# A two-layer sequence model on one core: block turns moved in front of the sums' emptying, value spreads in one pass of 128 rows, and a longer TensorE loop

## The chip, the cores and the metric

The kernel runs on one core of a Trainium2 chip. The metric is the device time of one execution in microseconds (us). The engines are TensorE (PE; its weight loads are PEld), VectorE (DVE), ScalarE (ACT), GpSimd (POOL) and SyncE (SP), which here only issues DMAs. Differences of less than 0.2% can't be told from no change.

## The reference, cut to what matters

`x` is 8 batches of 512 tokens of 128 numbers. Layer 0 adds a pairwise attention of 16 channels and a routed expert block to `x`; layer 1 adds a linear attention with a hierarchical state and a gated feed-forward block:

```
xn = layernorm(x)
# layer 0, for each of 16 channels c of 64 numbers:
u, v = xn @ U.T * s, xn @ V.T * s
q    = sigmoid(u_c @ v_c.T)                 # 512 x 512 scores
G    = concat(q @ v_c) @ U + concat(q.T @ u_c) @ V, times s
F    = for 8 experts: the 64 tokens with the best router logit,
       attention among them, added back at their places
x    = x + G + F
xn = layernorm(x)
# layer 1
k, q = elu(xn Wk)+1, elu(xn Wq)+1 ;  v = xn Wv
y    = sum over 7 groups of features f: D_f(q) * cumsum_t( A_f(k) * B_f(v) )
x    = x + (y / denominator) @ Wo
       + (silu(xn Wg) * (xn Wu)) @ Wd
```

A, B, C and D are multiplications by fixed 64 x 128 matrices ("spreads"): B spreads the values v. Products that must be exact are made from a high and a low part (`fp32r`): high x high, high x low, low x high.

## The kernel before, in words

A prologue loads and normalises all batches, computes the router logits and picks the tokens (0 to 88 us), then runs the experts (88 to 158 us). The first pair of channels of batch 0 is computed by itself in that time ("early").

The main part walks over batches. A batch is 8 pairs of channels (`j`), a pair is two halves (`o` = 0 and 1), so 16 halves, h = 0 to 15; even halves have `o` = 0. In each half TensorE does, in this order:

1. `scores`: four units, each 6 passes on 64 rows (u times v, 24 matmuls, two at a time on the two halves of the array), into eight PSUM banks. ACT turns each unit into `tanh` (L1172). Before the fourth unit TensorE waits (`s_oe`) until DVE has emptied the other sum's bank: in an odd half that is the sum of the even half just before.
2. the middle work, by a table: in even halves the next pair's u and v (`pu`, `pv`, 3 passes each) and the output projection of the last pair (`pj`, 6 passes); and steps of layer 1 of the batch before: the spreads (`ROWS`) and single steps (`FULL_STEPS`, both in the table at L69 to L75). A spread B stands alone in halves 4, 5 and 6 (`B0`, `B1`, `B2`), and beside a D later.
3. `weighted`: four units of `tok` times `tanh`, 16 fp32 matmuls, into the sum's bank (`o_bank`), which DVE then empties as high and low part (`evac_o`, L866 and L868).

`tok` is u and v of the pair with tokens on the partitions. It is made from `raw` (u and v, copied by ACT, L1121) by a DVE transposition of 32 x 32 blocks (`turn`, L789) into the single buffer `blocks`, and by 16 DMAs from SP that put the blocks in their places (`move_tokens`, L533). `turn` waits until the DMAs of the turn before have landed (`s_moved`), and the first `weighted` of the next pair waits for its own. In an even half the turn stands in DVE's order behind the emptying of that half's sum, which needs the last `weighted` of the half.

Batch 0 runs without layer 1 (halves 2 to 15) as straight code, batches 1 to 7 in a loop of one batch a pass (`pe.Fori(1, B)`), and then comes the tail: layer 1 of the last batch. The first pair that the main part needs (`turn(0, 0)`) goes the same way through a buffer of its own, `first_blocks`, at 155 us.

A second buffer name to know: layer 1's gate uses `tg`, which shares its place with `kexp` (the exponential of the step `kq`).

Of the kernel before, what the change touches and what calls it, by code (L numbers as in the profile page):

```python
# [35 lines left out]
ALU = mybir.AluOpType  # L36
# [3 lines left out]
P = 128  # L40
B, T, D = 8, 512, 128
TB = T // P
# [31 lines left out]
FULL_STEPS = {1: [("back", 0)], 2: [("norm", 0)], 3: [("kq", 0), ("v", 0)], 12: [("down", 0)], 15: [("yo", 0), ("yo", 1)]}  # L74
FULL_STEPS |= {h: [("gate", f), ("up", f)] for h, f in ((5, 0), (6, 1), (9, 2))}  # L75

# [124 lines left out]
def prep_index(g, k):  # L201


    return g * 2 + 3 + k
# [6 lines left out]
def build(nc, io):  # L211
    ctx = ExitStack()
    with ctx:
# [17 lines left out]
        def scatter_bank(i):  # L231
            return x_bank(("sc", 0), not isinstance(i, int))
# [18 lines left out]

        mv1, ve1, rstd1 = sb("mv1", [P, B, TB, 2]), sb("ve1", [P, B, TB]), sb("rstd1", [P, B, TB])
# [70 lines left out]
        wr_b = take_upper(B * (E * B + 1))  # L323
# [34 lines left out]
        first_blocks = view(arena[:, at[0] - 6 * T:at[0] - 4 * T], (2, T))  # L358
# [18 lines left out]
        later_blocks = sb("blocks", [P, 2, T])  # L377
# [17 lines left out]
        s_stats, s_rstd = sem("stats_ready"), sem("rstd_ready")  # L395
        s_xn, s_xT, s_xnT = sem("xn_ready"), sem("xn_transposed"), sem("xn1T_ready")
# [88 lines left out]
        def _(sp):  # L485
# [42 lines left out]
            def move_tokens(i, j, blocks):  # L528

                sp.wait_ge(s_turned, i * PAIRS + j + 1)  # L530
                for r in range(QUARTERS):
                    for a in range(QUARTERS):
                        sp.dma_start(tok[32 * r:32 * r + 32, (j + 1) % 2, :, :, 32 * a:32 * a + 32].rearrange("t w k c -> t (w k) c"),  # L533
                                     blocks[32 * a:32 * a + 32].rearrange("t w (k r c) -> t (w k) r c", k=TB, r=QUARTERS)[:, :, r])\
                          .then_inc(s_moved[j], 16)

            move_rows(E - 2, E // 2 - 1, 0)
            move_tokens(0, 0, first_blocks)
            move_rows(E - 1, E // 2 - 1, 1)

# [9 lines left out]
            load_rows(0)  # L550
            for j in range(1, PAIRS):
                move_tokens(0, j, later_blocks)
                if j == 2:
                    sp.wait_ge(s_yp, 1)
                    load_rows(1)

            def batch(n, more):
                for j in range(PAIRS):
                    move_tokens(n, j, later_blocks)
# [67 lines left out]
        def _(dve):  # L627
# [52 lines left out]
            def part_rows(h):  # L680
                dve.wait_ge(s_rstd, h + 1)
                for n in range(h * X_PART, (h + 1) * X_PART):
                    if n >= 2:
# [1077 lines left out]
```

## Time and profile before

| | us |
|---|---|
| median of 3 runs | 1463.75 (1462.65 to 1465.48) |
| the profiled execution | 1468.4 |
| its span (first to last instruction) | 1466.6 |
| batch 0, from the first score of half 2 | 157.93 to 294.93 |
| seven passes of the loop | 294.93 to 1413.70, 158.7 to 161.9 each |
| tail | 1413.70 to 1466.6 |

TensorE is busy in 95% of the span, DVE in 62%, ACT in 47%. Times in the rows are from the span's start. An idle time in brackets stands in front of the group it belongs to, and behind the arrow is what ended it; "issue" means that no other engine was waited for. Matmul ends are modelled, so the distance from start to start tells what a pass costs.

### The profile page before, as it was taken

The page shows a single profiled execution, that of the slowest core. Times are in us where ns is not written, and L with a number is a line of the kernel's source. Part 1 is how long each engine was busy: PE and PEld are TensorE (multiplying, and loading weights), DVE is VectorE, ACT ScalarE, POOL GpSimd, SP SyncE. Part 2 cuts the span into 40 slices and gives each one's busy share as a digit, 9 for nine tenths or more (in the row PEclk, how much of TensorE's full clock was granted, in tenths as well). Part 3 has the DMA queues.
Part 4 walks back from the last instruction along what each step waited for, and adds up shares of the span by engine and source line. Part 5 has one row for each costly group of instructions (what it writes and reads, how often), then busy time and mean ns, then how long its engine had stood idle before and what let it go on. Part 6 is the DMA issues. An engine that isn't in the chain of part 4 may idle for free.

```text
span 1466.6 us, 24503 instructions
## 1 busy us (share of the span) xinstructions
PE 1389.9 (95%) x7806; PEld 793.9 (54%) x7806; DVE 903.6 (62%) x1559; ACT 688.9 (47%) x1058; POOL 44.1 (3%) x41
## 2 busy tenths in 40 slices
PE   6999798899998999999999999999999999999968
PEld 3566444455564555555565555555655555555534
DVE  8868443366655665656655656556555666566657
ACT  3556344444443544454444543454544454454421
POOL 4000400000000000000000000000000000000000
PEclk9999899999999999999999999999999999999988
DMA  6012222112221212221112211221212111221110
GB/s 207 1 31 66 43 35 31 26 29 35 30 30 31 33 27 30 36 32 31 26 26 39 36 29 24 36 34 28 30 29 36 32 26 27 38 30 27 25 30 8
DMA packets 302620, 51.37 MB, mean 35 GB/s; under 512 B 280545, under 2 KB 300769, under 8 KB 302465
## 3 DMA queue, kind: packets, MB, share of 16 engines
q1 hardware_dynamic: 302128, 47.82, 19.4%
q8 instruction: 78, 1.28, 0.4%
q0 software_dynamic: 336, 1.64, 0.3%
q14 instruction: 78, 0.63, 0.2%
HBM read 11.64 MB, written 4.19 MB: 11 GB/s over the span
## 4 chain that ended last, share of the span: by engine, by line
issue 85%; DVE 1%; PE 1%; POOL 1%; ACT 0%; POOLq 0%; DVEq 0%
PE psum L1231 1%; DVE arena L917 0%; DVE arena L923 0%; DVE arena L915 0%; POOL u_w_hl L608 0%; POOL v_w_hl L608 0%; POOL rstd_s L623 0%; POOL up_hl L608 0%; DVE arena L939 0%; PE psum L1575 0%; DVE xn_s L663 0%; POOL u_w_hl L605 0%; POOL v_w_hl L605 0%; DVE x_all L932 0%; POOL up_hl L605 0%
## 5 line engine op out<-in xcount | busy, mean ns | idle before, releaser
L1172 ACT ACTIVATE arena<-psum 128x1024 f32<-128x1024 f32 x504 | 476.0, 1030 | 636.5 <-PE psum L1231 636.3
L1231 PE MATMUL psum<-arena 128*64 128x512 f32 x2016 | 466.0, 605 | 26.0 <-DMA arena<-blocks 14.6
L1231 PEld LDWEIGHTS psum<-arena 128*64 128x64 f32 x2016 | 135.0, 138 | 290.0 <-issue 244.7
L1231 PE MATMUL psum<-u_parts,v_parts 64*128 64x512 f32 x1536 | 199.5, 404 | 11.9 <-issue 11.2
L1231 PE MATMUL psum<-v_parts,u_parts 64*128 64x512 f32 (+1 forms) x1568 | 201.9, 397 | 0.0
L866 DVE TENSOR_SCALAR o_hl<-psum,sums 128x512 fp32r<-128x512 f32 x126 | 94.4, 749 | 162.1 <-PE psum L1231 162.1
L1231 PEld LDWEIGHTS psum<-u_parts,v_parts 64*128 64x128 f32 x1536 | 141.7, 187 | 93.1 <-issue 45.3
L1231 PEld LDWEIGHTS psum<-v_parts,u_parts 64*128 64x128 f32 (+1 forms) x1568 | 145.3, 184 | 81.5 <-issue 51.1
L868 DVE SCALAR_TENSOR_TENSOR o_hl<-psum,sums,o_hl 128x512 fp32r<-128x512 f32 x126 | 94.6, 751 | 4.5
L1121 ACT ACTIVATE arena<-psum 128x512 f32<-128x512 f32 x128 | 77.1, 625 | 18.5 <-PE psum L1231 18.5
L923 DVE TENSOR_TENSOR arena<-psum,arena 128x512 f32<-128x512 f32 x96 | 64.6, 689 | 33.7 <-PE psum L1231 31.7
L772 DVE CAST u_parts<-arena 128x512 fp32r<-128x512 f32 x64 | 28.7, 448 | 88.0 <-ACT arena L1121 88.0
L789 DVE STREAM_TRANSPOSE blocks<-arena 128x1024 f32<-128x1024 f32 x63 | 77.8, 1234 | 0.0
L917 DVE TENSOR_TENSOR_SCAN arena<-ones,arena 128x512 f32<-128x512 f32 x56 | 68.6, 1224 | 1.9
L915 DVE TENSOR_TENSOR arena<-psum,arena 128x512 f32<-128x512 f32 x32 | 22.1, 691 | 63.0 <-PE psum L1231 36.4
L1231 PE MATMUL psum<-sel_r,uT_hl 128*128 128x512 f32 x189 | 60.5, 428 | 0.0
L1231 PE MATMUL psum<-o_hl,u_w_hl 128*128 128x512 f32 x189 | 54.0, 394 | 1.7 <-DVE o_hl L868 1.7
L1231 PE MATMUL psum<-sel_r,vT_hl 128*128 128x512 f32 x189 | 54.5, 396 | 0.0
L1231 PE MATMUL psum<-o_hl,v_w_hl 128*128 128x512 f32 x189 | 53.2, 389 | 0.0
L1231 PE MATMUL psum<-arena,top_w 128*64 128x512 f32 x96 | 49.3, 595 | 1.5 <-DVE arena L923 1.5
L1231 PE MATMUL psum<-arena,bot_w 128*64 128x512 f32 x96 | 49.3, 595 | 0.0
L773 DVE TENSOR_TENSOR u_parts<-arena,u_parts 128x512 fp32r<-128x512 f32 x64 | 46.5, 727 | 2.2
(211 smaller groups left out, 1517.0 us busy)
## 6 DMA issues: line engine op xcount, KB each, us to landing
arena<-blocks SPq DMA_DIRECT2D x1008, 32.0 KB, 2.0
x_all<-in_x SPq DMA_DIRECT2D x4, 512.0 KB, 5.4
upper<-in_we SPq DMA_DIRECT2D x8, 256.0 KB, 2.7
expert_rows<-upper SPq DMA_DIRECT2D x16, 128.0 KB, 2.5
xn_s<-expert_rows SPq DMA_DIRECT2D x8, 256.0 KB, 2.9
out<-x_all SPq DMA_DIRECT2D x8, 256.0 KB, 2.5
arena<-in_e POOLq DMA_DIRECT2D x1, 896.0 KB, 5.7
arena<-in_wi POOLq DMA_DIRECT2D x1, 576.0 KB, 5.7
```

Of the source, the lines that this page charges most:

```text
L772: link(nc.vector.tensor_copy(hl[:, par, 0], raw[:]))
L773: return nc.vector.tensor_tensor(hl[:, par, 1], raw[:], hl[:, par, 0], ALU.subtract)
L789: nc.vector.transpose(blocks.rearrange("p w t -> p (w t)"), raw.rearrange("p w t -> p (w t)")).then_inc(s_turned, 1)
L866: nc.vector.tensor_scalar(o_hl[:, o, 0], o_bank[o][:], total, None, ALU.add).then_inc(s_oh, 1)
L868: nc.vector.scalar_tensor_tensor(o_hl[:, o, 1], o_bank[o][:], total, o_hl[:, o, 0], ALU.add, ALU.subtract)\
L915: nc.vector.tensor_tensor(ab[:], bk[:], bs_of(f)[:], ALU.mult).then_inc(s_ld, 1)
L917: link(nc.vector.tensor_tensor_scan(pre[:], ones[:], ab[:], 0.0, ALU.mult, ALU.add))
L923: nc.vector.tensor_tensor(pc[half][:, r % 2], bk[:], pre[:], ALU.mult).then_inc(s_ld, 1)
L1121: nc.scalar.activation(raw[:], bk[:], ACT.Copy, accum_out=total[:, par:par + 1]).then_inc(s_prep_free, 1)
L1172: nc.scalar.activation(th_of(un), psum[:, at:at + 2], ACT.Tanh, scale=0.5 * FACTOR_SCALE ** 2).then_inc(s_th, 2)
L1231: return nc.tensor.matmul(out, lhsT, rhs, start=start, stop=stop)
```

## The change

Seven edits go together.

1. In an even half `turn` now stands in front of `evac_o`.
2. The two tiles of the first pair of the main part are made by eight TensorE transpositions (`prep` with k = 3 and 4) and two ACT copies (`prep_tok`) instead of `turn(0, 0)` and 16 DMAs; `first_blocks` goes.
3. A lone B spread is one pass over 128 rows: the low part of v is written to rows 64 to 127 of `val_high`, whose weights are the same as those of rows 0 to 63. B2 keeps a second pass for the low part of the weights. The subtraction that makes the low part becomes two of 64 rows.
4. The first gate and up step move from half 5 to half 3, behind `kq` and `v`.
5. TensorE's loop has two batches in its body and runs three times; batch 1 is straight code in front of it. The other engines' loops stay.
6. In the prologue ACT normalises the odd batches (`odd_rows`), DVE the even ones.
7. The router logits of two batches go into column groups 0 to 31 and 64 to 95 with 32 output rows each, instead of 64 rows for one batch.

```diff
-FULL_STEPS = {1: [("back", 0)], 2: [("norm", 0)], 3: [("kq", 0), ("v", 0)], 12: ...
-FULL_STEPS |= {h: [("gate", f), ("up", f)] for h, f in ((5, 0), (6, 1), (9, 2))}
+FULL_STEPS = {1: [("back", 0)], 2: [("norm", 0)], 3: [("kq", 0), ("v", 0), ("gate", 0), ("up", 0)], 12: ...
+FULL_STEPS |= {h: [("gate", f), ("up", f)] for h, f in ((6, 1), (9, 2))}
...
             def part_rows(h):
                 dve.wait_ge(s_rstd, h + 1)
-                for n in range(h * X_PART, (h + 1) * X_PART):
-                    ...
-                    normalised(xn_g[:, n % 2], n, ...).then_inc(s_xn, 1)
+                odd, even = h * X_PART + 1, h * X_PART
+                nc.vector.scalar_tensor_tensor(shift1[:, odd], mv1[:, odd, :, 0], -1.0, rstd1[:, odd], ALU.mult, ALU.mult)\
+                  .then_inc(s_shift, 1)
+                if h:
+                    dve.wait_ge(s_xT, even - 1)
+                normalised(xn_g[:, 0], even, ...).then_inc(s_xn, 1)
...
-            def turn(i, j, blocks):
-                if not (isinstance(i, int) and i == j == 0):
-                    dve.wait_ge(s_moved[(j - 1) % PAIRS], (i + (j > 0)) * MOVED)
+            def turn(i, j):
+                if not (isinstance(i, int) and i == 0 and j == 1):
+                    dve.wait_ge(s_moved[(j - 1) % PAIRS], moved_count(i if j else i - 1, (j - 1) % PAIRS))
...
-            dve.wait_ge(s_prep_w, 1)
-            turn(0, 0, first_blocks)
             expert_rows(E - 1, 1, E // 2 - 1)
...
                 elif kind == "v":
                     dve.wait_ge(s_vh, L + 1)
-                    nc.vector.tensor_tensor(val_parts[1][:], bk[:], val_parts[0][:], ALU.subtract).then_inc(s_ld, 1)
+                    nc.vector.tensor_tensor(val_parts[0][64:128], bk[64:128], val_parts[0][64:128], ALU.subtract)
+                    nc.vector.tensor_tensor(val_parts[1][0:64], bk[0:64], val_parts[0][0:64], ALU.subtract).then_inc(s_ld, 1)
...
+                    if o == 0:
+                        if not some_before:
+                            for n in range(2):
+                                dve.wait_ge(s_ymv[n], 16 * E)
+                        turn(i, j)
                     evac_o(g, j, o, some_before)
                     for r in range(ROUNDS):
                         ...
-                    if o == 0:
-                        ...
-                        turn(i, j, later_blocks)
...
+            def odd_rows(n):
+                act.wait_ge(s_shift, n // 2 + 1)
+                if n >= 2:
+                    act.wait_ge(s_xT, n - 1)
+                for k in range(TB):
+                    ins = nc.scalar.activation(xn_g[:, 1, k], x_all[:, n, k], ACT.Identity, bias=shift1[:, n, k:k + 1],
+                                               scale=rstd1[:, n, k:k + 1])
+                ins.then_inc(s_xna, 1)
...
+            def prep_tok(k, w, bk):
+                act.wait_ge(s_prep_full, prep_index(0, k) + 1)
+                copy(tok[:, 1, w].rearrange("p k c -> p (k c)"), bk[:]).then_inc(s_prep_free, 1)
...
-                return mm(bank[2][0:E * B], wr_b[:, n * E * B:(n + 1) * E * B], xn1T[:, n], n == 0, n == B - 1)
+                for g in range(2):
+                    ins = mm(bank[2][g * 64:g * 64 + 32], wr_b[:, pair * 32:pair * 32 + 32], xn1T[:, 2 * pair + g],
+                             pair == 0, pair == B // 2 - 1)
...
+                if len(group) == 1 and group[0][0] == "B":
+                    f, bk = group[0][1], banks[0]
+                    ins = mm(bk[:], e_high[:, (NF + f) * P:(NF + f + 1) * P], val_parts[0][:], True, f < 2)
+                    if f >= 2:
+                        ins = mm(bk[:], e_low[0:64, ...], val_parts[0][0:64], False, True)
+                    ins.then_inc(s_lf, 1)
+                    return
...
             probabilities_back(*last)
+            prep(0, 3, 1, 0, bank[2])
             attend(*last)
+            prep(0, 4, 1, 0, bank[3])
             expert_out(*last)
...
-            with pe.Fori(1, B) as i:
-                iteration(i, True, True)
+            iteration(1, True, True)
+            with pe.Fori(1, B // 2) as m:
+                for n in range(2):
+                    iteration(m * 2 + n, True, True)
```

DVE's order at the end of half 4 of a batch in the loop, before (u and v parts of the next pair, the projection's sum, the emptying of the sum in two instructions, the turn):

```order
L773 TENSOR_TENSOR v_parts<-arena,v_parts 128x512
L858 SCALAR_TENSOR_TENSOR arena<-psum,arena 128x512
L863 ISA
L866 TENSOR_SCALAR o_hl<-psum,sums 128x512
L867 REGISTER_ALU
L868 SCALAR_TENSOR_TENSOR o_hl<-psum,sums,o_hl 128x512
L789 STREAM_TRANSPOSE blocks<-arena 128x1024
```

The same place with the change:

```order
L783 TENSOR_TENSOR v_parts<-arena,v_parts 128x512
L866 SCALAR_TENSOR_TENSOR arena<-psum,arena 128x512
L798 REGISTER_ALU
L799 STREAM_TRANSPOSE blocks<-arena 128x1024
L871 ISA
L874 TENSOR_SCALAR o_hl<-psum,sums 128x512
L875 REGISTER_ALU
L876 SCALAR_TENSOR_TENSOR o_hl<-psum,sums,o_hl 128x512
```

The turn is now the instruction in front of the two that empty the sum.

TensorE's order in the middle of half 5, before (from the scores' last unit to the first `weighted`):

```order
L1231 MATMUL psum<-v_parts,u_parts 128x512 x6
L1465 REGISTER_ALU
L1231 MATMUL psum<-val_high,e_high 128x512
L1231 MATMUL psum<-val_low,e_high 128x512
L1465 REGISTER_ALU
L1231 MATMUL psum<-kq_high,e_high 128x512 x2
L1231 MATMUL psum<-kq_low,e_high 128x512 x2
L1231 MATMUL psum<-sel_r,gate_hl 128x512 x3
L1465 REGISTER_ALU
L1231 MATMUL psum<-sel_r,up_hl 128x512 x3
L1231 MATMUL psum<-arena 64x512 x6
```

and with the change:

```order
L1265 MATMUL psum<-v_parts,u_parts 128x512 x6
L1509 REGISTER_ALU
L1265 MATMUL psum<-val_high,e_high 128x512
L1509 REGISTER_ALU
L1265 MATMUL psum<-kq_high,e_high 128x512 x2
L1265 MATMUL psum<-kq_low,e_high 128x512 x2
L1583 REGISTER_ALU
L1265 MATMUL psum<-arena 64x512 x6
```

The pass of `val_low` has gone, and the six passes of gate and up stand in half 3 behind those of `kq` and `v`.

## Rows read from the trace of the kernel before

**Rows 1.** The page's first part: busy us, share of the span, instructions.
```profile
PE 1389.9 (95%) x7806; PEld 793.9 (54%) x7806; DVE 903.6 (62%) x1559; ACT 688.9 (47%) x1058; POOL 44.1 (3%) x41
```

**Rows 2.** Waits of TensorE: who waited for what, us in total, times, longest.
```profile
PE psum L1231 <- DMA arena<-blocks: 14.6, 16, 2.3
...
PE psum L1231 <- issue: 11.2, 7, 2.2
...
PE psum L1231 <- DMA arena<-arena: 5.5, 1, 5.5
...
PE psum L1231 <- DVE val_low L911: 2.7, 1, 2.7
```

**Rows 3.** Timeline, half 0 of batch 4: start, us, engine, line, operation.
```profile
784.59 0.68 DVE L858 SCALAR_TENSOR_TENSOR arena<-psum,arena 128x512 f32<-128x512 f32 x1
...
787.15 0.75 DVE L866 TENSOR_SCALAR o_hl<-psum,sums 128x512 fp32r<-128x512 f32 x1 [1.87 <-PE psum L1231]
...
788.60 1.23 DVE L789 STREAM_TRANSPOSE blocks<-arena 128x1024 f32<-128x1024 f32 x1
```

**Rows 4.** Timeline of batch 3: a train of block DMAs on SP's queue.
```profile
708.10 10.86 SPq L533 DMA_DIRECT2D arena<-blocks  x16
```

**Rows 5.** Timeline of batches 0 and 2: `weighted` behind a short and two long waits.
```profile
262.83 3.65 PE L1231 MATMUL psum<-arena 128*64 128x512 f32 x16 [0.98 <-DMA arena<-blocks]
...
282.08 5.35 PE L1231 MATMUL psum<-arena 128*64 128x512 f32 x16 [2.06 <-DMA arena<-blocks]
...
462.84 4.49 PE L1231 MATMUL psum<-arena 128*64 128x512 f32 x12 [2.28 <-DMA arena<-blocks]
```

**Rows 6.** Timeline: the first scores of batches 2 and 4.
```profile
454.56 3.02 PE L1231 MATMUL psum<-u_parts,v_parts 64*128 64x512 f32 x24 [1.56 <-issue]
...
775.99 4.22 PE L1231 MATMUL psum<-u_parts,v_parts 64*128 64x512 f32 x24 [2.17 <-issue]
```

**Rows 7.** Timeline, end of half 4 of batch 4.
```profile
819.85 0.69 DVE L915 TENSOR_TENSOR arena<-psum,arena 128x512 f32<-128x512 f32 x1 [3.80 <-ACT arena L1027]
...
824.56 0.68 DVE L858 SCALAR_TENSOR_TENSOR arena<-psum,arena 128x512 f32<-128x512 f32 x1
824.83 3.03 PE L1231 MATMUL psum<-v_parts,u_parts 64*128 64x512 f32 x24
825.16 0.74 DVE L866 TENSOR_SCALAR o_hl<-psum,sums 128x512 fp32r<-128x512 f32 x1
```

**Rows 8.** Timeline of TensorE, half 8 of batch 3: passes on 64 and on 128 rows.
```profile
696.69 0.39 PE L1231 MATMUL psum<-kq_low,e_high 64*128 64x512 f32 x2
696.91 0.39 PE L1231 MATMUL psum<-kq_high,e_low 64*128 64x512 f32 x2
697.23 0.97 PE L1231 MATMUL psum<-sel_r,uT_hl 128*128 128x512 f32 x3
```

**Rows 9.** Timeline of DVE, half 3 of batch 4.
```profile
813.52 0.68 DVE L911 TENSOR_TENSOR val_low<-psum,val_high 128x512 fp32r<-128x512 f32 x1
814.51 0.75 DVE L866 TENSOR_SCALAR o_hl<-psum,sums 128x512 fp32r<-128x512 f32 x1 [0.31 <-PE psum L1231]
```

**Rows 10.** Timeline of TensorE, an odd half of batch 0 without middle work.
```profile
252.26 3.65 PE L1231 MATMUL psum<-arena 128*64 128x512 f32 x16 [0.97 <-ACT arena L1172]
```

**Rows 11.** Timeline around half 2 of batch 0, all engines.
```profile
164.08 1.91 DVE L772 CAST u_parts<-arena 128x512 fp32r<-128x512 f32 x1 [4.71 <-ACT arena L1121]
...
167.58 1.36 DVE L773 TENSOR_TENSOR v_parts<-arena,v_parts 128x512 fp32r<-128x512 f32 x1
...
168.82 5.88 PE L1231 MATMUL psum<-arena 128*64 128x512 f32 x16 [5.45 <-DMA arena<-arena]
174.63 3.06 PE L1231 MATMUL psum<-v_parts,u_parts 64*128 64x512 f32 x24
```

**Rows 12.** Timeline of the prologue: one batch's logits, and the router's exponential.
```profile
21.80 1.07 PE L1231 MATMUL psum<-xn1T,upper 128*64 128x512 f32 x2
...
26.95 0.59 ACT L1036 ACTIVATE arena<-psum 64x512 f32<-64x512 f32 x1 [1.17 <-PE psum L1231]
```

More of the change, by code:

```diff
@@ L231, in scatter_bank @@
         def scatter_bank(i):
-            return x_bank(("sc", 0), not isinstance(i, int))
+            return x_bank(("sc", 0), not (isinstance(i, int) and i == 0))
         x_all = sb("x_all", [P, B, TB, D])
@@ L527, in _ @@
                 move_rows(E - 4 + par, E // 2 - 2, par)
[L528 to L539, printed above, removed]
+            for par in range(2):
+                move_rows(E - 2 + par, E // 2 - 1, par)
             def load_rows(n):
@@ L1008, in iteration @@
                             add_y(r, i - 1)
-                    if o == 0:
-                        if not some_before:
-                            for n in range(2):
-                                dve.wait_ge(s_ymv[n], 16 * E)
-                        turn(i, j, later_blocks)
             iteration(0, True, False)
@@ L1032, in transposed @@
                 copy(xn1T[:, n], bank[par][:]).then_inc(s_xnT, 1)
-            pairs(fori_of(act), transposed)
+            def odd_rows(n):
[6 more added lines that the diff above has]
+                ins.then_inc(s_xna, 1)
+            odd_rows(1)
+            for n in range(0, B, 2):
+                transposed(n, 0)
+                transposed(n + 1, 1)
+                if n + 3 < B:
+                    odd_rows(n + 3)
             act.wait_ge(s_lg, 1)
-            nc.scalar.activation(tk_work, bank[2][0:E * B], ACT.Exp, scale=-1.0).then_inc(s_ex, 1)
+            for g in range(2):
+                ins = nc.scalar.activation(tk_work[g * 32:g * 32 + 32], bank[2][g * 64:g * 64 + 32], ACT.Exp, scale=-1.0)
+            ins.then_inc(s_ex, 1)
             act.wait_ge(s_first, 16 * len(first_consts))
@@ L1117, in prep_raw @@
                     act.wait_ge(s_us if k == 1 else s_vs_rdy, g + 1)
-                    act.wait_ge(s_turned, g)
+                    if isinstance(g, int) and g == 1:
+                        act.wait_ge(s_prep_full, prep_index(0, 4) + 1)
+                    else:
+                        act.wait_ge(s_turned, g - 1)
                 if q is not None:
@@ L1233, in _, with transposes @@
             pe.wait_ge(s_first, 16 * len(first_consts))
-            def transposes(n, par):
-                pe.wait_ge(s_xn, n + 1)
-                if later(n):
+            def transposes(n):
+                par = n % 2
+                if par == 0:
+                    pe.wait_ge(s_xn, n // 2 + 1)
+                else:
+                    pe.wait_ge(s_xna, n // 2 + 1)
+                if n >= 2:
                     pe.wait_ge(s_xnT, n - 1)
@@ L1482, in prep @@
                     ins = product(bk, uv_hl[k - 1], pair, xn1_hl)
+                else:
+                    pe.wait_ge(s_prep_free, prep_index(g, k - 2) + 1)
+                    for t in range(TB):
+                        ins = nc.tensor.transpose(bk[:, t * P:(t + 1) * P], (u_raw if k == 3 else v_raw)[:, t * P:(t + 1) * P],
+                                                  ident[:])
                 ins.then_inc(s_prep_full, 1)
```

84 lines of the change are left out of this document (51 added, 33 removed).

## The prediction

> **What bounds the kernel now.** I read the page's first part, then TensorE's waits, then the timeline of every place that the change touches. TensorE is busy in 95% of the span [rows 1]: what the change gives or takes is what it does to TensorE's passes and pauses. In the list of its waits the reader is to see four lines [rows 2]: 14.6 us in 16 waits for block DMAs, 11.2 us in 7 waits for nothing but issue (a short one in the prologue, and six at turns of the loop, some 10.9 together), one wait of 5.5 us for the first pair's DMAs, and one of 2.7 us in the tail. A wait can cost more than itself: 16 `weighted` matmuls take 3.65 us after a wait of 0.98, but 5.35 after one of 2.06, and 12 of them take 4.49 after one of 2.28 [rows 5]; the granted clock falls, to the lower of its levels at worst. The pauses that the change aims at are some 34 us, or 2.3%. What a measurement of this kernel can tell from no change is 0.2%, 3 us.
>
> **Part 1, the turn in front.** In half 0 DVE is done at 785.2 and stands idle 1.87 us for the last `weighted`, empties the sum in two instructions, and turns at 788.60 [rows 3]. The turn needs only `raw`, which was there before. In front it runs in that pause, costs TensorE nothing, and starts 3.4 us earlier. Its train of 16 DMAs takes 10.86 us to issue [rows 4] and about 2 more to land, so it ends as much earlier. The longest wait is 2.28 us [rows 5], so all 16 should go: 14.6 us, and the slow stretches behind the waits of 2.06 and 2.28 with them, 5.35 - 3.65 = 1.7 and 4.49 - 2.65 (12 matmuls at full clock) = 1.8. Term: -18.
>
> One even half is different. In half 4 DVE waits 3.80 us for ACT's copy of B0, and from there works without a pause: `add_g` starts at 824.56, the emptying 0.60 behind it at 825.16, when the half has been over since 824.83 [rows 7]. Here the turn finds no pause; it puts the two emptying instructions off by some 1.2, to end at 827.9 instead of 826.7. Behind them TensorE waits with the fourth unit of half 5. That unit begins 18 matmuls, 9 pairs of 0.227, into the half, at 826.9. So a stall of 1.0 to 1.3, I take 1.15, once in each of seven batches: +8.0. Below it can be nothing (if DVE gets ahead), above 1.5.
>
> **Part 2, the first pair on TensorE.** The wait of 5.45 us at 168.82 goes, and the slow 5.88 becomes 3.65 [rows 11]: 7.7 in all. The eight transpositions (about 0.6 us for four) stand in two gaps of 0.7 each where TensorE waits for ACT at the last expert; they cost nothing there, at worst 1.2. But something else comes late. DVE's parts of the next pair, which wait for nobody before, take 1.91 to 1.36 us each beside POOL's work and end only at 168.94 [rows 11]; the half would now end near 167. Turn and emptying stand behind them: emptied at about 171.8, while the fourth unit of half 3 wants it at 169.1. A stall of 2.7 is given back. Term: -5, between 0 and -7.7.
>
> **Part 3, the lone B.** A pass lasts 0.22 us (696.69 to 696.91) [rows 8]. Three passes a batch less would be 0.67. But a 128-row pass now stands between 64-row passes. The row shows the price of changing from 64 to 128 rows: 0.32 instead of 0.22 from 696.91 to 697.23 [rows 8]. B0 and B1 each get one such change more, and one back, which no row shows; I take the same 0.1 for it, between 0 and 0.2. They then save 0.03 each, and B2, which stands before 128-row passes anyway, 0.22: together 0.28 a batch, 2.0 in seven. The Trainium skill, "TensorEngine Tiling (Array Packing)", Key Properties, says that changing the tiling mode drains the array; by free passes the term would be 4.7, by this rule nearer to 2, and the trace's 0.1 agrees with the rule. The second subtraction on DVE is counted next.
>
> **Part 4, gate and up in half 3.** Six passes of 0.23, 1.4 us, leave half 5 and enter half 3: no change in the sum, if both halves stay filled. Half 5 then has three short passes between scores and `weighted`, about 1.1 us with the changes; an odd half with nothing there waits 0.97 for the third tanh [rows 10], so it is just full. In half 3 DVE's chain grows by three instructions. From the subtraction at 813.52 [rows 9] I count 0.6, 0.6 and 0.7 to the next starts, so up starts near 815.4 and ends near 816.1. The emptying, which started at 814.51 as soon as the half was over [rows 9], could now start at 815.9 (1.4 later) and has to wait for up until 816.1. It ends at 817.6; the fourth unit of half 4 wants it 2.04 into the half, at 817.8. The move costs nothing, and 0.5 a batch (3.5) if my count is short. Half 5's stall from part 1 isn't hidden by this. Terms of parts 3 and 4: -2.
>
> **Part 5, the longer loop.** Six turns back cost 10.9 us of pause: 1.56 and 2.17 are two of them, and behind the second the scores take 4.22 instead of 3.02 [rows 6]. With batch 1 in front and two batches a pass there are two turns back left, four go: 4 x 1.8 = 7.3, and perhaps one slow stretch (1.3). Straight code shows no such pauses: batch 0 is straight and has none between its halves. Term: -8 (7.3 and half of that stretch), between 0 and -10. A body twice as long could make each of the two turns dearer; the Trainium skill, "Runtime: NRT & Kernel Launch", Instruction fetch mechanics, says that a taken branch outside a small window forces a fetch of its target, whatever the length of the body. By that rule the price goes with the number of turns, which is what I take from the row.
>
> **Parts 6 and 7, the prologue.** From 20 us on each batch takes 1.59 us of TensorE (the next logits start 1.59 later), 1.07 of it the logits [rows 12]. Two batches' logits side by side in two column groups would take 1.07 for both. But ACT now has the odd rows too (four activations, near 1.2) and the last statistics come at 17 us and through POOL at 18.6. I follow the chain: last even rows at 20.0, odd at 21.4, copies at 22.8, logits at 24.0, two exponentials to 25.2, where it was 27.54 (26.95 + 0.59) [rows 12]. DVE's search for the best tokens and the early pair both start from there. Term: -2.5, between 0 and -4.
>
> **The tail.** TensorE waits 2.7 us for `val_low` [rows 2]; the six passes of gate and up now fill it, and 1.3 us of DVE work leave the chain behind. Against it stands one subtraction more, 0.6. Term: -1.5, between +0.7 and -3.
>
> **The sum.** -18 + 8 - 5 - 2 - 8 - 2.5 - 1.5 = -29. The profiled execution took 1468.4 (span 1466.6) and would take 1439. The runs' median is 4.65 below that execution; from 1463.75 the sum gives 1434.75, I say 1435.
>
> **Rivals.**
> *The trains stay the limit.* If the DMAs, not the turn, decide (one buffer `blocks`, trains that follow each other), only half of the 18 comes: 1444. For it: a train with its landing is 13 us of the 17 to 22 of a pair. Against it: a pause of 4 us or more between trains. 10%.
> *The chain in halves 3 to 5 is dearer.* DVE late in half 3 too (+3.5) and stalls of 1.5 (+2.4), with no gain from the lone B (+2): 1443. For it: half 4 has no slack at all [rows 7]. 15%.
> *Better.* The stall in half 5 is absorbed, and the prologue and the first pair give their full: 1435 - 8 - 1.5 - 2.7 = 1423. Against it: the chain of rows 7 is all DVE's own work. 10%.
> *Slower.* The turn stands in front of the emptying in every even half, 63 of them. If DVE came to it less than about 0.8 us before the half's end everywhere, as in half 4, TensorE's fourth unit would stall 0.95 (1.24 of turn less 0.3 of slack) in the 56 others too: +53, less my 29: 1488. It decides from the point where DVE's last work ends later than that. In half 0 it ends 1.87 before [rows 3], and only half 4 fails: 3%.
> *The longer body doesn't help* (its two turns cost as much as six): 1443. Only the total of 10.9 speaks for a fixed price. 7%.
>
> **How the numbers follow.** My forecast has 55%, with a range of its own of 1428 to 1441. The cases at 1443 and 1444 have 32%, the better one 10%, the slower 3%. Eight in ten lie between 1423 and 1448. All but the slower case and a little unknown are faster by more than 0.2%: faster 0.94, same 0.02, slower 0.04.
>
> **What would show it.** In the profile after: waits of TensorE for blocks gone or under 2 us; two waits called issue near 2 us in the loop, not six; turns that end before the emptying starts; in half 5 a gap in the scores before the fourth unit, near 1.1 us, in each batch; no wait at half 2 of batch 0, but one in half 3; the first exponential near 24; batches of about 158. I am wrong if block waits remain, if the scores of odd halves other than 5 are stretched, or if the pauses at the loop's two turns grow past 4.

## The result, and the profile after

| | before | after |
|---|---|---|
| median of 5 runs each | 1464.23 us (1462.65 to 1468.57) | 1454.76 us (1454.3 to 1455.87) |
| ratio, 95% interval | | 0.9931 (0.9917 to 0.9946) |
| span of the profiled execution | 1466.6 | 1453.3 |
| start of half 2 of batch 0 | 157.93 | 155.64 |
| batch 0 | 137.00 | 124.67 |
| from there to the last half of batch 7 | 1109.40 | 1113.09 |
| what follows | 62.27 | 59.90 |

The change gains 9.5 us, not the 29 forecast; 1454.76 lies above the forecast's own range of 1428 to 1441. The start, batch 0 and the end gain 17.0 us of the span. The loop, where seven eighths of the work are, loses 3.7. Places within the execution are read from one profiled execution of each kernel.

First the parts of the page and the list of TensorE's waits after (us in total, times, longest), which answer to [rows 1, 2]:

```profile
PE 1387.6 (95%) x7790; PEld 785.1 (54%) x7790; DVE 903.1 (62%) x1554; ACT 698.2 (48%) x1077; POOL 44.7 (3%) x41
```

```profile
PE psum L1265 <- DVE o_hl L876: 12.9, 13, 3.5
PE psum L1265 <- issue: 8.1, 5, 2.3
...
PE psum L1265 <- DVE val_low L920: 1.4, 1, 1.4
```

No wait for block DMAs is left: 14.6 and 5.5 us are gone. New is the first line, 13 waits for the sum's emptying. "issue" fell only from 11.2 to 8.1, though four of six turns of the loop went.

Half by half (start of the first score to start of the next half's), summed over batches 1 to 7 (half 15: 1 to 6), after minus before. A half 15 so ends with the pause of the turn behind it, if there is one; the six passes of gate and up that moved make nearly all of half 3's +9.54.

```
half 0: -0.92   half 1: +6.37   half 3: +9.54   half 4: +1.55   half 5: -4.16
half 6: +1.32   half 8: -3.37   half 15: -7.79
```

Four things are new in them. First, TensorE's turn of the loop in the changed kernel (timeline of TensorE at the first scores of batches 4 and 6; the idle time in front of a group stands in brackets):

```profile
758.12 0.49 PE L1265 MATMUL psum<-u_parts,v_parts 64*128 64x512 f32 x1 [2.03 <-issue]
760.86 5.22 PE L1265 MATMUL psum<-u_parts,v_parts 64*128 64x512 f32 x23 [2.24 <-issue]
...
1080.58 0.49 PE L1265 MATMUL psum<-u_parts,v_parts 64*128 64x512 f32 x1 [1.26 <-issue]
1083.34 4.46 PE L1265 MATMUL psum<-u_parts,v_parts 64*128 64x512 f32 x23 [2.27 <-issue]
```

Each turn pauses twice, with one score between, and the 23 scores behind take 5.22 and 4.46 us where 24 took 3.02 [rows 6]. The granted clock was 0.50 from 758.8 to 765.6 and from 1083.3 to 1086.4, its lower level. Half 0 of those two batches takes 14.45 and 13.71 us, of the others 9.50.

Second, half 1 of the batches in which TensorE does not turn (timeline of batch 2, DVE and then TensorE):

```profile
442.47 0.69 DVE L961 TENSOR_TENSOR arena<-xn_s,arena 128x512 f32<-128x512 f32 x1 [3.03 <-issue]
...
448.70 1.23 DVE L799 STREAM_TRANSPOSE blocks<-arena 128x1024 f32<-128x1024 f32 x1
449.86 0.71 DVE L874 TENSOR_SCALAR o_hl<-psum,sums 128x512 fp32r<-128x512 f32 x1
450.60 0.75 DVE L876 SCALAR_TENSOR_TENSOR o_hl<-psum,sums,o_hl 128x512 fp32r<-128x512 f32 x1
```

```profile
448.84 1.67 PE L1265 MATMUL psum<-v_parts,u_parts 64*128 64x512 f32 x12 [0.59 <-DVE arena L866]
451.41 0.96 PE L1265 MATMUL psum<-v_parts,u_parts 64*128 64x512 f32 x6 [0.90 <-DVE o_hl L876]
```

DVE's own loop still turns once a batch, with an idle time of 3.03 us for "issue". From there it works without a pause to the emptying of half 0's sum, and TensorE waits for it. Before, DVE had the same pause (14.8 us in six), but TensorE paused in the same place in each batch, and half 1 took 8.97 everywhere. Now it takes 11.05, 10.38, 10.36 and 10.42 in batches 2, 3, 5 and 7.

Third, the lone B. Timeline of TensorE in half 4 of batch 4, before and after, from the pass of `val_high` to the first pass on 128 rows:

```profile
817.26 0.39 PE L1231 MATMUL psum<-val_high,e_high 64*128 64x512 f32 x1
817.49 0.39 PE L1231 MATMUL psum<-val_low,e_high 64*128 64x512 f32 x1
817.55 0.56 PE L1231 MATMUL psum<-kq_high,e_high 64*128 64x512 f32 x2
817.88 0.46 PE L1231 MATMUL psum<-kq_low,e_high 64*128 64x512 f32 x2
```

```profile
804.32 0.50 PE L1265 MATMUL psum<-val_high,e_high 128*128 128x512 f32 x1
804.75 0.50 PE L1265 MATMUL psum<-kq_high,e_high 64*128 64x512 f32 x2
805.09 0.40 PE L1265 MATMUL psum<-kq_low,e_high 64*128 64x512 f32 x2
805.41 0.97 PE L1265 MATMUL psum<-sel_r,uT_hl 128*128 128x512 f32 x3
```

Read the distances of starts. From 817.26 the 128-row pass of `sel_r` is 1.01 away, with `val_high` 0.22 behind the last score: 1.235 in all. After, the one pass starts 0.32 behind the last score, the next (64 rows) 0.43 behind it, then 0.34 and 0.32: 1.41. One pass less, and 0.17 us more.

B2 in half 6, which keeps a second pass of 64 rows, has the same changes of height (batch 4, after):

```profile
823.45 0.50 PE L1265 MATMUL psum<-val_high,e_high 128*128 128x512 f32 x1
823.88 0.50 PE L1265 MATMUL psum<-val_high,e_low 64*128 64x512 f32 x1
824.32 0.97 PE L1265 MATMUL psum<-sel_r,gate_hl 128*128 128x512 f32 x3
```

Its last step, from 64 rows back to 128, costs 0.44 here and not 0.32. From the last score to `sel_r` it is 1.18 us, before 1.00.

Fourth, half 5 (batch 4, DVE and TensorE), the stall that was forecast:

```profile
812.11 1.23 DVE L799 STREAM_TRANSPOSE blocks<-arena 128x1024 f32<-128x1024 f32 x1
813.27 0.71 DVE L874 TENSOR_SCALAR o_hl<-psum,sums 128x512 fp32r<-128x512 f32 x1
814.01 0.75 DVE L876 SCALAR_TENSOR_TENSOR o_hl<-psum,sums,o_hl 128x512 fp32r<-128x512 f32 x1
814.89 0.96 PE L1265 MATMUL psum<-v_parts,u_parts 64*128 64x512 f32 x6 [0.58 <-DVE o_hl L876]
```

In batch 0 the wait of [rows 11] has moved, as forecast, from half 2 to half 3: halves 2 and 3 together take 21.07 us instead of 24.30.

```profile
166.13 0.87 DVE L783 TENSOR_TENSOR v_parts<-arena,v_parts 128x512 fp32r<-128x512 f32 x1
...
166.93 1.23 DVE L799 STREAM_TRANSPOSE blocks<-arena 128x1024 f32<-128x1024 f32 x1
...
168.09 0.70 DVE L874 TENSOR_SCALAR o_hl<-psum,sums 128x512 fp32r<-128x512 f32 x1
...
168.83 0.75 DVE L876 SCALAR_TENSOR_TENSOR o_hl<-psum,sums,o_hl 128x512 fp32r<-128x512 f32 x1
169.63 1.65 PE L1265 MATMUL psum<-v_parts,u_parts 64*128 64x512 f32 x6 [3.52 <-DVE o_hl L876]
```

### The profile page after: what moved, and what is told of

Read it like the earlier page. It is cut to its first block, busy times and chain, and to the rows that moved or that the text cites. A ratio compares the mean times of both kernels' runs of the same rounds, so it can differ in the third digit from the quotient of the medians.

```text
span 1453.3 us, 24349 instructions
## 1 busy us (share of the span) xinstructions
PE 1387.6 (95%) x7790; PEld 785.1 (54%) x7790; DVE 903.1 (62%) x1554; ACT 698.2 (48%) x1077; POOL 44.7 (3%) x41
## 4 chain that ended last, share of the span: by engine, by line
issue 86%; DVE 2%; POOL 1%; PE 1%; ACT 0%; POOLq 0%; DVEq 0%
PE psum L1265 1%; DVE arena L926 1%; DVE arena L924 0%; DVE arena L932 0%; POOL v_w_hl L614 0%; POOL u_w_hl L614 0%; POOL rstd_s L629 0%; DVE arena L948 0%; PE psum L1634 0%; DVE xn_s L669 0%; POOL u_w_hl L611 0%; POOL v_w_hl L611 0%; POOL up_hl L614 0%; DVE x_all L941 0%; POOL gate_hl L611 0%
## 5 line engine op out<-in xcount | busy, mean ns | idle before, releaser
L1265 PE MATMUL psum<-v_parts,u_parts 64*128 64x512 f32 (+1 forms) x1568 | 207.9, 402 | 11.7 <-DVE o_hl L876 11.1
```

The lines of the kernel that those rows point to most:

```text
L1265: return nc.tensor.matmul(out, lhsT, rhs, start=start, stop=stop)
```

## The experiments

All ratios are to runs of the kernel before on the same chip; its medians there lie between 1463.9 and 1465.2 us. "Edit 1" to "edit 7" are the numbers of the list of the change.

### The parts alone

**b_turn**: before, with edit 1 alone.

```diff
+                    if o == 0:
+                        turn(i, j, later_blocks)
                     evac_o(g, j, o, some_before)
...
-                    if o == 0:
-                        turn(i, j, later_blocks)
```

> The kernel before with edit 1 alone (the turn in front of the emptying). Theory: the 16 waits for blocks and the slow stretches behind two of them go (-18), half 5 of each batch gets a stall before its fourth unit (+8, at 1.15 each), and half 1 gets none, because TensorE's own turn of the loop still covers DVE's: 1454. Rival: the turn in front is itself what ate the gain, by emptying sums late in many halves: 1460 or more, with stalls behind o_hl in halves other than 5.

Measured: 1453.18 us, ratio 0.9911 (0.9883 to 0.9938). Half 0 gives 10.0 us, half 8 3.4, batch 0 5.8; half 5 goes from 9.07 to 10.11 (+7.3 in seven). That is 12 us of gain for this edit: all seven edits together bring no more than the first one alone (9.5 us; the two intervals overlap). Half 1 costs 1.0 in all, nearly all of it in batch 2 (9.93), where DVE's own pause at its turn was 3.17: the cover by TensorE's pause is not complete.

**a_noB**: after, with edit 3 undone (the single subtraction and the passes of `val_high` and `val_low`).

```diff
-                    nc.vector.tensor_tensor(val_parts[0][64:128], bk[64:128], val_parts[0][64:128], ALU.subtract)
-                    nc.vector.tensor_tensor(val_parts[1][0:64], bk[0:64], val_parts[0][0:64], ALU.subtract).then_inc(s_ld, 1)
+                    nc.vector.tensor_tensor(val_parts[1][:], bk[:], val_parts[0][:], ALU.subtract).then_inc(s_ld, 1)
...
-                if len(group) == 1 and group[0][0] == "B":
+                if False:
```

> The changed kernel with edit 3 undone (a lone B again in two or three passes of 64 rows). Theory: a 128-row pass between 64-row passes costs two changes of mode (0.31 and 0.43 where 0.22 stood) and 0.11 more on the pass behind, so the edit lost 0.18 to 0.2 us at each of 21 places: undoing it gives -4, 1451. Rival, the forecast's price: the edit saved 0.28 a batch, undoing it costs 2: 1457.

Measured: 1440.42 us, ratio 0.9823 (0.9797 to 0.9848), 14 us better than after. The lone B itself explains 2.5 of them (half 4 -1.43, half 6 -1.26, half 5 +0.22). Half 0 gives 9.15, and neither expectation had that: the second pauses were gone. The start (153.25 instead of 155.64) gives 2.4, about the spread of the start from profile to profile.

```profile
753.11 3.02 PE L1264 MATMUL psum<-u_parts,v_parts 64*128 64x512 f32 x24 [1.85 <-issue]
...
1070.00 3.02 PE L1264 MATMUL psum<-u_parts,v_parts 64*128 64x512 f32 x24 [1.35 <-issue]
```

No instruction at the turn differs; the code ahead of it, and the body in halves 4 to 6, are of another length.

**a_loop1**: after, with edit 5 undone.

```diff
-            iteration(1, True, True)
-            with pe.Fori(1, B // 2) as m:
-                for n in range(2):
-                    iteration(m * 2 + n, True, True)
+            with pe.Fori(1, B) as i:
+                iteration(i, True, True)
```

> The changed kernel with edit 5 undone (TensorE's loop again of one batch, seven passes). Theory: the edit gained nothing, since its two turns have two pauses each and a slow stretch, and DVE's own turn of the loop, which TensorE's used to cover, now stalls half 1 (1.4 to 2.1 in four batches); undoing it: the excess of halves 15, 0 and 1 goes from 19 to about 14, so 1450, and no stall in half 1. Rival, the forecast's term: four pauses come back and nothing else: +8, 1463.

Measured: 1446.18 us, ratio 0.9857 (0.9827 to 0.9886). The longer loop costs 8.6 us: half 0 -9.07 and half 1 -5.88 when it goes, half 15 +6.83. Six pauses of 1.29 to 1.95 us are back, none of them double. This is the price of the longer loop at the place that it has in the changed kernel. Where the second pauses are away (a_pad128, a_pad64 and a_pad16 below: 1445.1, 1445.5 and 1442.9 us), the longer loop is about even with a_loop1: batches 1 to 7 up to the last half take 1105.5, 1103.4 and 1104.2 us, in a_loop1 1104.9. What TensorE saves in half 15 (6.8 here), DVE's turn takes back in half 1 (5.9).

**a_gate5**: after, with edit 4 undone.

```diff
-FULL_STEPS = {..., 3: [("kq", 0), ("v", 0), ("gate", 0), ("up", 0)], ...
-FULL_STEPS |= {h: [("gate", f), ("up", f)] for h, f in ((6, 1), (9, 2))}
+FULL_STEPS = {..., 3: [("kq", 0), ("v", 0)], ...
+FULL_STEPS |= {h: [("gate", f), ("up", f)] for h, f in ((5, 0), (6, 1), (9, 2))}
```

> The changed kernel with edit 4 undone (gate and up of the first group again in half 5). Theory: the six passes only change their half: half 3 back to 8.15, half 5 near 10, total within 1 us of 1455. Rival: the move made DVE late in half 3 and so cost half 4 its 0.2 us a batch: undoing it gives 1453 and half 4 back at 10.42.

Measured: 1462.85 us (10 runs), ratio 0.9983 (0.9969 to 0.9996). Both expectations missed. Half 5 gets longer by 11.35 us when the passes come back, half 3 shorter by only 4.69 (9.51 to 8.83, not to 8.15). DVE in half 3 shows why:

```profile
799.09 0.69 DVE L919 TENSOR_TENSOR val_high<-psum,val_high 64x512 fp32r<-64x512 f32 x1
799.80 0.68 DVE L920 TENSOR_TENSOR val_low<-psum,val_high 64x512 fp32r<-64x512 f32 x1
800.41 0.73 DVE L874 TENSOR_SCALAR o_hl<-psum,sums 128x512 fp32r<-128x512 f32 x1
```

The second subtraction of edit 3 stands, undelayed, ahead of the emptying; with gate and up in the half the time is there, without them it isn't. And the turns took another form again, one pause of double length each, which stands between the weight load of the first score and the score (the first line is the weight load):

```profile
757.50 0.18 PEld L1265 LDWEIGHTS psum<-u_parts,v_parts 64*128 64x128 f32 x1 [2.85 <-issue]
760.51 5.44 PE L1265 MATMUL psum<-u_parts,v_parts 64*128 64x512 f32 x24 [4.98 <-issue]
...
1085.46 5.12 PE L1265 MATMUL psum<-u_parts,v_parts 64*128 64x512 f32 x24 [4.40 <-issue]
```

### The turns of the loops

**a_pad128**: after, with 128 waits that are already met at the head of TensorE's program.

```diff
+            for _ in range(128):
+                pe.wait_ge(s_ones, 1)
             pe.wait_ge(s_first, 16 * len(first_consts))
```

> The changed kernel with 128 waits that are already met put at the head of TensorE's program, where it waits for the first rows anyway; nothing else changes but the place of TensorE's loop in its code. Theory: the second pause behind each of the two turns (2.24 and 2.27 us after the first score, with a slow stretch behind) hangs on where the loop's first instructions lie in the blocks in which code is fetched; half 0 of batches 4 and 6 goes from 14.45 and 13.71 to about 9.5: -9, 1446. Rival: it is the length of the body: nothing changes, 1455.

Measured: 1445.11 us, ratio 0.987 (0.9852 to 0.9888). Waits that do nothing make the kernel 9.6 us faster. The pauses are 1.86 and 1.81, single; behind the first of them the clock still falls once (half 0 of batch 4 takes 11.06), so half 0 gives 7.6 here and 9.1 with 64 or 16 waits.

**a_pad64** and **a_pad16**: the same with 64 and 16 waits (one run each).

> Edit: the changed kernel with 64 waits that are already met at the head of TensorE's program (128 of them took the second pauses at the turns away, 1445 us). Nothing else moves but the place of the loop in memory. Theory: the pause at a turn depends on where the turn's target and what follows it lie; so this place gives pauses of its own: the first of 1.3 to 2.2 us, the second either 2.2 us or nothing, by the place; 1445 or 1454 us. Rival: any shift by whole steps takes the second pauses away, then they were an accident of the one place: 1445 us.

> Edit: the changed kernel with 16 waits that are already met at the head of TensorE's program. By the theory that the place alone decides, a small shift moves which instruction the second pause stands at, or leaves all as it is: TensorE then stops again in front of a score near the 23rd of the last 24 of half 0, and 16 instructions earlier or later; 1454 us. Rival: the place doesn't matter and the pauses are those of the changed kernel without any shift of the instruction that waits.

Measured: 1445.5 and 1442.9 us. No second pause in either; the first ones are 1.41 and 1.53, 1.98 and 1.93 us. My expectation for a_pad16 was wrong: every shift tried takes the second pauses away. This is a_pad64:

```profile
756.10 3.02 PE L1265 MATMUL psum<-u_parts,v_parts 64*128 64x512 f32 x24 [1.41 <-issue]
...
1073.92 3.02 PE L1265 MATMUL psum<-u_parts,v_parts 64*128 64x512 f32 x24 [1.53 <-issue]
```

The Trainium skill, "Runtime: NRT & Kernel Launch", Instruction fetch mechanics, says that instructions are fetched in blocks of 256. The traces agree and show the pauses' cause. One DMA queue, `q8 instruction`, carries packets of 16,384 bytes, two around each turn of TensorE; a_dve2, which changes DVE's loop alone, leaves them where they are. This is the second one in after (window 758.3 to 759.6), then in a_pad64 (756.2 to 757.5):

```profile
q8 instruction: 1, 0.02, 6.0%
...
q8 instruction: 1, 0.02, 5.9%
```

From the start of the first score of batch 4 (in brackets batch 6), start and end of these packets in the packed traces, in us:

| | first packet ends | second packet | further stop of TensorE |
|---|---|---|---|
| after | -1.93 (-1.80) | 0.23 to 1.48 (0.35 to 1.27) | between first and second score |
| a_pad64 | -1.94 (-1.89) | 0.16 to 1.40 (0.22 to 1.75) | none |
| a_gate5 | -4.99 (-4.57) | -2.78 to -1.48 (-2.43 to -1.25) | between the first weight load and the first score |

In all three the second packet starts 0.6 to 0.8 us behind TensorE's first instruction of the new pass. In a_pad64 nothing needs it yet. In after the second score stands until 2.74 (2.76), 1.26 (1.49) us behind the packet's end: the block ends right behind the first score. The counts of instructions agree. Ahead of the first score of batch 2 the trace of after has 4662 instructions of TensorE, weight loads, waits and register instructions included; a_gate5 has one more, and its stop stands one instruction earlier; a_noB has six more, as many as stand from the loop's first instruction to the first score, and has no second stop. (Not every wait that is met at once leaves a record: of a_pad16's 16 the trace shows 8.) So a loop whose first instructions lie at the end of a block needs two blocks at once and pays for both. The Trainium skill, in the same section, calls the crossing into the next block mostly hidden; behind a turn it took 2.24 and 2.27 us.

**a_dve2**: after, with DVE's loop over two batches like TensorE's, so that both turn in the same batches.

```diff
-            loop(1, B, LINKS, body)
+            body(1)
+            def two(m):
+                body(m * 2)
+                body(m * 2 + 1)
+            loop(1, B // 2, 2 * LINKS, two)
```

> The changed kernel with DVE's loop, too, of two batches a pass and batch 1 in front. Theory: half 1 of batches 2, 3, 5 and 7 lasts 10.4 to 11.1 instead of 8.98 because DVE's own turn (2.8 to 3.0 us idle) delays its chain, turn and emptying; with the turn gone there, -6.4: 1448. Rival: DVE was late for its work (scatter, parts) and not for its loop: 1455, half 1 unchanged.

Measured: 1449.3 us, ratio 0.99 (0.9882 to 0.9917). Half 1 is 8.98 in every batch, -6.3 us. TensorE's program isn't touched, and its double pauses stay (1.67 and 2.24, 1.75 and 2.56).

**a_unroll**: after, with TensorE's and DVE's batches 1 to 7 written out.

```diff
-            with pe.Fori(1, B // 2) as m:
-                for n in range(2):
-                    iteration(m * 2 + n, True, True)
+            for n in range(2, B):
+                iteration(n, True, True)
...
-            loop(1, B, LINKS, body)
+            for n in range(1, B):
+                body(n)
```

> The changed kernel with the loops of TensorE and DVE written out in full. Theory: all pauses called issue at batches' ends go (halves 15, 0 and 1: 3.4, 9.2 and 6.4), 19 in all: 1436. Rival: code that runs straight for 1.2 ms is fetched too slowly at places and brings pauses of its own: over 1440.

Measured: 1435.89 us, ratio 0.9805 (0.9786 to 0.9824). No pause called issue over 0.2 us is left in either engine's batches. The gain is 18.9 us, and the halves at the turns give as much (half 15 -3.4, half 0 -9.2, half 1 -6.3). Straight code of seven batches streams without a stop.

### Better versions

**best1**: a_unroll with edit 3 undone, as in a_noB.

> As the one before, with the lone B in passes of 64 rows again. Theory: another -2.7 from halves 4 and 6 and up to 1 in the tail: 1433. Rival (the 128-row pass saves where no loop blurs it): 1438.

Measured: 1430.9 us, ratio 0.9782 (0.9756 to 0.9808). Against a_unroll half 4 gives 2.1, half 6 1.05 and half 5 costs 0.8: 2.3 in the loop, as in a_noB (2.5), now with no turn in the way. The medians differ by 5.0. The rest is the tail (1.5) and the start (0.5), and both vary as much between profiles of kernels with the same code there: in the seven with the lone B the tail takes 59.8 to 62.1 us. So 2.3 to 2.5 is what the rows show as the price of the lone B.

**best2**: best1 with two exceptions to the turn in front.

```diff
-                        turn(i, j)
-                    evac_o(g, j, o, some_before)
+                        if not (second and j == 2) and some_before:
+                            turn(i, j)
+                    if some_before or o:
+                        evac_o(g, j, o, some_before)
+                    if o == 0 and ((second and j == 2) or not some_before):
+                        turn(i, j)
...
                         elif work[0] == "pv":
+                            if not (some_before or o):
+                                evac_o(g, j, o, some_before)
                             prep_v(g, (j + 1) % 2)
```

> Edit: the version best1 (1430.9 us: the changed kernel with TensorE's and DVE's batches written out and edit 3, the one pass of 128 rows, undone), and two exceptions to the turn in front: in half 4 of batches 1 to 7 the emptying stands in front of the turn again, and in half 2 of batch 0 it stands in front of v's parts of the next pair and of the turn. Theory: in half 4 DVE has no pause, so the turn there only delays the emptying, and TensorE pays it with 0.78 us before the fourth unit of half 5, seven times (5.5 us); in half 2 of batch 0 the emptying stands behind 1.6 us of v's parts and 1.2 us of turn, and of the stall of 3.50 us in half 3 only about 1 stays, with the slow weighted matmuls behind it (5.35 instead of 3.65 us) gone too, some 4 us. Expected 1422 us (1420 to 1425). Rival: the transfer of half 4 is then late for half 6, or the stall in half 3 is made by the last copies of the prologue and not by the order: no gain, 1430 or above.

Measured: 1429.39 us, ratio 0.9761 (0.9747 to 0.9774); expected was 1422. Half 5 falls to 7.65 in all seven batches (-6.0), as expected. In batch 0 the stall in half 3 went down to 0.81, and the transfer came too late instead:

```profile
166.07 0.96 PE L1271 MATMUL psum<-v_parts,u_parts 64*128 64x512 f32 x6 [0.81 <-DVE o_hl L876]
...
168.08 1.23 DVE L799 STREAM_TRANSPOSE blocks<-arena 128x1024 f32<-128x1024 f32 x1
...
181.66 2.83 PE L1271 MATMUL psum<-arena 128*64 128x512 f32 x6 [5.10 <-DMA arena<-blocks]
```

I had priced the stall and not the train behind the turn. The turn comes 2.0 us later in the half than in best1 (13.34 against 11.30), and without the stall the `weighted` of half 4 are wanted 4.3 us earlier. It is the very wait that edit 1 had removed elsewhere.

**best3**: the same for half 4; in half 2 of batch 0 turn and emptying stand in front of both parts.

```diff
                         elif work[0] == "pu":
+                            if not some_before:
+                                dve.wait_ge(s_prep_free, prep_index(g, 2) + 1)
+                                for n in range(2):
+                                    dve.wait_ge(s_ymv[n], 16 * E)
+                                turn(i, j)
+                                evac_o(g, j, o, some_before)
                             prep_u(g, g + 1 if some_before else None, (j + 1) % 2)
```

> Edit: best1 again with two exceptions to the turn in front: in half 4 of batches 1 to 7 the emptying stands in front of the turn (as in best2, where it took 6.0 us out of half 5), and in half 2 of batch 0 the turn and behind it the emptying now stand in front of both parts of the next pair. In best2 the turn of that half came behind v's parts and the emptying; the stall of 3.50 us in half 3 went down to 0.81, but a wait of 5.10 us for the block DMAs came in half 4. Theory: the turn needs only the raw copies, which are there at 158.9; it then ends near 160.2, its transfer is under way before the next one is wanted, and the emptying starts when the half is over. No stall in half 3, no wait in half 4: batch 0 gets 3.5 us and the slow stretch of weighted matmuls (1.7 us) shorter than in best1, the loop 6. Expected 1420 us (1418 to 1423). Rival: the parts of the next pair, which DVE makes beside POOL's work in 1.6 to 2.7 us each, come too late for the scores of half 4, and the stall only moves there; 1424 us.

Measured: 1421.99 us (1421.5 to 1423.65), ratio 0.9706 (0.9691 to 0.9721), the best version: 42.9 us under the kernel before on the same chip, 4.5 times the gain of the change. Timeline of half 2 and 3 of batch 0:

```profile
159.62 1.25 DVE L799 STREAM_TRANSPOSE blocks<-arena 128x1024 f32<-128x1024 f32 x1 [4.62 <-ACT arena L1156]
...
161.73 3.04 PE L1272 MATMUL psum<-v_parts,u_parts 64*128 64x512 f32 x24
161.85 0.75 DVE L874 TENSOR_SCALAR o_hl<-psum,sums 128x512 fp32r<-128x512 f32 x1 [0.98 <-PE psum L1272]
...
165.72 3.65 PE L1272 MATMUL psum<-arena 128*64 128x512 f32 x16 [0.95 <-ACT arena L1211]
```

No stall in the scores, `weighted` at full speed, and half 3 takes 7.58 us instead of the 12.95 of after.

## Why the prediction was wrong

The direction was right, and so was the part that gives most. The sum failed at one term with its sign and its size, and at a smaller one in the same way.

**The step that failed: part 5, the longer loop, forecast -8, measured +8.6** (a_loop1). The term said "With batch 1 in front and two batches a pass there are two turns back left, four go". On TensorE that came: with the program shifted by 64 waits, half 0 is 9.5 everywhere, only the two first pauses of 1.41 and 1.53 stay, and half 15 takes 8.1 us less than before. Two things were missing.

- A turn has no fixed price, and the cost doesn't go with the number of turns alone: one that needs two blocks of code pays twice. I took 1.8 from six rows of one loop at one place. At the place that the change gives it, each turn costs a second pause of 2.2 us, the wait for a second block of code, and scores 1.4 to 2.2 us slower at the lower clock: +9.1 us by two of three shifts that change nothing else, +7.6 by the third. That the loop came to lie there is an accident of the length of the code in front of it. "If the pauses at the loop's two turns grow past 4" was the right test, and read as sums (2.03 + 2.24 = 4.27 and 1.26 + 2.27 = 3.53) it fell at one of the two. The rival "The longer body doesn't help" had the right object and a cap at nothing gained; neither it nor I let the turns lose.
- DVE turns too. I looked for pauses in TensorE's list alone. DVE's 14.8 us of "issue" in six were in its own list, and cost nothing as long as TensorE paused beside them. Edit 5 takes that cover away in four batches of six: +6.4 in half 1, shown by a_dve2 (-6.3) from DVE's side and by a_loop1 (-5.9) from TensorE's. This part is no accident: at a good place of the loop it alone leaves next to nothing of the forecast 8 us (a_pad128, a_pad64 and a_pad16 against a_loop1).

**Part 3, the lone B, forecast -2 with the gate's move, measured +2.3 to +2.5 by itself.** "One such change more, and one back, which no row shows; I take the same 0.1 for it, between 0 and 0.2". Back is dearer: the 64-row pass behind a 128-row pass starts 0.43 later instead of 0.22, and the one behind it again 0.11 late. That is 0.3 for the way back, above my upper bound of 0.2, and more than a pass of 0.23 that it saves. And B2 was taken to save a full 0.22, because "B2, which stands before 128-row passes anyway"; but its second pass on 64 rows stands between, so it changes twice more, too, and loses 0.18. The rule of the Trainium skill that a change of the tiling mode drains the array ("TensorEngine Tiling (Array Packing)", Key Properties) points the right way; it has no price.

**Part 4, the gate's move.** Without the lone B it is worth 1.6 (a_noB against b_turn: half 3 +9.6, half 5 -11.2). With it, it is worth 6.7 in halves 3 and 5 (a_gate5), mostly because it hides the extra subtraction (0.68 in seven batches, 4.8). I had counted DVE's chain in half 3 with gate and up, not what the subtraction alone does.

**Part 1, forecast -18 + 8, measured -12 (b_turn).** All 16 waits went, slow stretches with them. The stall in half 5 is 1.04 a batch where I had 1.15; in after, with the gate's move, some 0.85 is left of it (8.49 against 7.65 in best2). Here the forecast named where the edit itself does harm; best2 and best3 take that harm out.

**Part 2, forecast -5, measured -3.2**, with the stall of 3.52 in half 3 where 2.7 was forecast: DVE's `v_parts` ended at 167.0, and turn and emptying behind it at 169.6. The turn in front of the emptying is part of that delay.

**Parts 6 and 7, forecast -2.5.** The router's exponentials of after end at 27.27, against 27.54 before, not at 25.2: the logits of two pairs come together at the end.

```profile
24.12 1.91 PE L1265 MATMUL psum<-xn1T,upper 128*32 128x512 f32 x8
...
26.08 1.19 ACT L1060 ACTIVATE arena<-psum 32x512 f32<-32x512 f32 x2 [1.25 <-PE psum L1265]
```

That pair of kernels alone would say "no gain". But the start of half 2 is 153.1 to 155.6 in the twelve profiles with this prologue (mean 154.05) and 157.93 and 156.10 in the two with the old one: 3.0 better, with a spread of 2.5 from profile to profile. Size right within that spread, as far as two old profiles tell; the steps are not shown, and edit 2, which also works ahead of that point, wasn't taken apart from them.

**The tail, forecast -1.5, measured -2.4** in these two profiles; the wait for `val_low` is 1.4 instead of 2.7. Over the seven profiles with the changed tail it takes 60.9 in the mean, against 62.3 and 62.2 in the two of before: -1.4, with a spread of 2.3.

The parts as measured (-12.0, -3.2, +2.5, -1.6, +8.6, -3.0, -1.4) add up to -10; the change measured -9.5. They were measured in different kernels, so the agreement is a rough one.

What stays open: why a first pause is 1.2 us at one turn and 2.2 at another; what inside the array makes the passes behind a change of height late; and a lone B that stands beside other 128-row passes, which wasn't tried. Halves 15 of 9.77 and 9.00 in after, against 7.67 without a turn, are not open: they are the first pauses of 2.03 and 1.26.

## What to carry to other kernels

A pause of one engine at a loop's turn can cover the same pause of another (here all but some 1 us of 6): count "issue" in every engine's list before giving one loop fewer turns, and do it for all or for none. The price of a turn depends on where its target lies in the program, so where two versions differ in length ahead of a loop, compare the turns' pauses first and take their difference out. And where work moves ahead on an engine in order, ask at each place whether the engine has a pause there; where it has none, leave the old order.

## What the runs showed of the hardware that was not expected

- A turn of TensorE's loop cost a pause of 1.19 to 2.17 us where one block of code was waited for. Where the block ended within the loop's first six instructions it cost 3.5 to 4.3 in two pieces (after, a_dve2) or 4.40 to 4.98 in one (a_gate5). The 16 instructions without effect ahead of the loop in a_pad16 took the second piece away.
- The turn of DVE's loop cost 2.36 to 3.17 us in the nine kernels that keep its loop of one batch, and 2.41 and 2.45 in a_dve2.
- Seven batches of straight code, 1,100 us of TensorE with DVE's own straight code beside it, ran without a pause at any batch's end (a_unroll and the three versions after it).
- From the start of a pass on 128 rows to that of one on 64 rows behind it lie 0.43 us, between two passes on 64 rows 0.22 to 0.23. The other way round it is 0.32 behind several passes on 64 rows, and 0.44 behind a single one that itself follows a pass on 128 rows.
